# x's second load issued at the exponential, and the stage back to channels on four quarters with two staging buffers and eight banks

## The chip, the cores and the metric

One core of one Trainium2 chip runs the whole program in one launch. The metric is the device time in microseconds (us); lower is better. The kernel before was timed in three runs.

## The reference, cut to what matters

The input x has 16 images of 128 channels of 32 x 32. The first layer normalises x in groups, takes each of the 16 x 128 matrices of 32 x 32 through a matrix logarithm, subtracts the mean logarithm, and takes the matrix exponential. The result is added to x itself; then attention with the 32 largest scores and a gated set of four experts follow on the tokens.

```python
x = x + _L0_conv_ref(_gn(x), L0_conv_gamma, L0_conv_beta)
t = _to_tokens(x)
t = t + _L1_attn_ref(_ln_t(t), ...)
t = t + _L1_ffn_ref(_ln_t(t), ...)
x = _from_tokens(t, x)
```

The change lies at the plus sign of the first line: the exponentials are laid out by 32 x 32 blocks, x by channels, and the stage called back to channels turns the first into the layout of the second and adds.

## The kernel before, in words

The program is a row of blocks; each block gives every engine its own list of instructions, and all engines meet at its end before the next one starts. The order is: constants, normalise, spectral constants, into blocks, eigen, take the logarithm (to line 764), exponential (lines 777 to 955), back to channels (lines 958 to 1008), load the weights (POOL's fills at lines 1109 to 1115, loads at line 1132), attention and experts.

Two large tiles of 128 partitions x 16 x 1024 floats (8 MB each) carry the first layer. `mem.odd` holds x, then the matrices under work, then the logarithms, and at the end the exponentials. `mem.even` holds the normalised x and then the eigenvectors; its last readers are lines 715 and 731, in the logarithm. From there to the stage back to channels nothing touches it.

**The exponential.** 128 tiles of 128 x 128 floats pass through a pipeline of ten steps on TensorE (line 951, each a set of sixteen 32 x 32 products), with ScalarE emptying the banks (line 916) and VectorE making the sums (lines 862 to 890). The helper `through` writes out the first 11 slots and the last ones instruction by instruction and puts the middle into a loop. SyncE issues two small loads there, gamma and beta (lines 831 and 832), and is then idle until the end of the block. VectorE's first instruction waits for both loads, its loop over tiles for POOL's small unit matrices (line 842).

**Back to channels.** SyncE issues the load of x from memory into `mem.even` (line 972) at the stage's start. Then a loop over four quarters (four images each):

- ScalarE copies a quarter of `mem.odd`, 128 x 4096 floats, rearranged into `stage[0]` (line 981), and then waits until TensorE has turned all eight banks of the quarter.
- TensorE waits for the copy and turns it in 32 products of 128 x 128 with the identity, four to a bank (line 993). Each float32 product shows in the trace as two weight loads and two matmuls, so a quarter is 64 of each. It uses banks 0 to 3 in turn: from the fifth bank on it waits until VectorE has added the bank four before. At the end of a quarter it waits for all eight adds.
- VectorE waits for the load of x once, and then for each bank (line 1003), and adds the bank, 128 x 512, to the matching part of `mem.even` (line 1007).
- POOL waits for the load of x (line 976).

`mem.work` has room for two quarters; only the first is used as a stage. PSUM has eight banks.

Lines 2105 to 2107 call the two stages:

```python
exponential(nc, mem, dram["gamma"], dram["beta"])
mem.work = first.enter_context(nc.sbuf_tensor("work2", [P, 2, HB * PAIRS * S], F32))
back_to_channels(nc, mem, x_dram)
```

The program's only engine with a queue for its own transfers here is SyncE; the profile calls instructions of that queue SPq. Instructions themselves are brought in by transfers too, which the profile lists as queues of the kind "instruction" (q8 and q14).

Of the kernel before, what the change touches and what calls it, by code (L numbers as in the profile page):

```python
# [12 lines left out]
P = 128  # L13
B = 16
S = 32
# [8 lines left out]
QUADS = B // 4  # L24
# [26 lines left out]
def hold(eng, sem, value):  # L51

    eng.wait_ge(sem, value)
    eng.sem_inc(Passed.sem, 1)


class Passed:
    sem = None
# [14 lines left out]
def constants(nc, mem):  # L73

    with ExitStack() as ctx:
        filled = ctx.enter_context(nc.semaphore("filled"))
        block = ctx.enter_context(nc.Block())

        @block.gpsimd
        def _(pool):  # L80
            nc.gpsimd.memset(mem.ident[:], 0.0).then_inc(filled, 1)
            nc.gpsimd.memset(mem.group[:], 1.0 / (GROUP * N)).then_inc(filled, 1)
            nc.gpsimd.memset(mem.quad_mean[:], 0.0).then_inc(filled, 1)
            nc.gpsimd.memset(mem.eps_gn[:], EPS_GN).then_inc(filled, 1)
            hold(pool, filled, 4)
            nc.gpsimd.affine_select(out=mem.ident[:], in_=mem.ident[:], compare_op=ALU.not_equal, fill=1.0,
                                    base=0, pattern=[[-1, P]], channel_multiplier=1).then_inc(filled, 1)

            gv = mem.group[:].rearrange("p (g c) -> p g c", c=GROUP)
            nc.gpsimd.affine_select(out=gv, in_=gv, compare_op=ALU.is_ge, fill=0.0, base=0,  # L90
                                    pattern=[[-GROUP, P // GROUP], [0, GROUP]], channel_multiplier=1).then_inc(filled, 1)
            hold(pool, filled, 6)
            nc.gpsimd.affine_select(out=gv, in_=gv, compare_op=ALU.is_ge, fill=0.0, base=GROUP - 1,
                                    pattern=[[GROUP, P // GROUP], [0, GROUP]], channel_multiplier=-1).then_inc(filled, 1)

            for d in range(-3, 4):
                hold(pool, filled, 7 + d + 3)
                nc.gpsimd.affine_select(out=mem.quad_mean[:], in_=mem.quad_mean[:], compare_op=ALU.not_equal,
                                        fill=1.0 / (B * P), base=S * d, pattern=[[-1, P]],
                                        channel_multiplier=1).then_inc(filled, 1)  # L100
# [673 lines left out]
EXP_LEAD = EXP_DEPTH + 2  # L774


def exponential(nc, mem, gamma_dram, beta_dram):


    with ExitStack() as ctx:  # L780
        def sem(name):
            return ctx.enter_context(nc.semaphore(name))
# [11 lines left out]
        loaded, step, eyes = sem("gb_loaded"), sem("exp_step"), sem("eyes")  # L794
# [4 lines left out]
        banks = [b[:, 0:EXP_W] for b in mem.banks]  # L799
        logs = mem.odd[:].rearrange("p m n -> p (m n)")  # L800
        block = ctx.enter_context(nc.Block())
        c = TAYLOR
# [26 lines left out]
        @block.sync  # L829
        def _(sp):  # L830
            sp.dma_start(scal[:, 0:1], gamma_dram.partition_broadcast(P)).then_inc(loaded, 16)
            sp.dma_start(scal[:, 1:2], beta_dram.partition_broadcast(P)).then_inc(loaded, 16)

        @block.gpsimd
        def _(pool):
# [119 lines left out]
            through(pe, slot)  # L955


def back_to_channels(nc, mem, x_dram):

    with ExitStack() as ctx:  # L960
        def sem(name):
            return ctx.enter_context(nc.semaphore(name))

        loaded, staged, turned, added = sem("x_again"), sem("back_staged"), sem("back_turned"), sem("back_added")
        stage = [mem.work[:, n].rearrange("p (c k) -> p c k", k=P) for n in range(2)]
        powers = mem.odd[:].rearrange("p (g b) n -> p g (b n)", g=QUADS)
        banks = mem.banks
        block = ctx.enter_context(nc.Block())

        @block.sync  # L970
        def _(sp):
            sp.dma_start(mem.even[:], x_dram).then_inc(loaded, 16)

        @block.gpsimd
        def _(pool):
            hold(pool, loaded, 16)

        @block.scalar
        def _(act):
            with act.Fori(0, QUADS) as g:  # L980
                nc.scalar.activation(stage[0].rearrange("p c k -> p k c"),
                                     powers[:, g, :].rearrange("p (k c) -> p k c", c=S), ACT.Copy).then_inc(staged, 1)
                act.wait_ge(turned, g * 8 + 8)

        @block.tensor
        def _(pe):
            with pe.Fori(0, QUADS) as g:
                hold(pe, staged, g + 1)
                for b in range(8):
                    if b >= 4:  # L990
                        hold(pe, added, g * 8 + b - 3)
                    for n in range(4):
                        last = nc.tensor.matmul(banks[b % 4][:, P * n:P * n + P], stage[0][:, 4 * b + n, :], mem.ident[:],
                                                start=True, stop=True)
                    last.then_inc(turned, 1)
                hold(pe, added, g * 8 + 8)

        @block.vector
        def _(dve):
            dve.wait_ge(loaded, 16)  # L1000
            with dve.Fori(0, QUADS) as g:
                for b in range(8):
                    dve.wait_ge(turned, g * 8 + b + 1)

                    d = mem.even[:, bass.ds(g * 4, 4), :].rearrange("p q (r c) -> p q r c", c=S)[:, :, :, 4 * b:4 * b + 4]
                    d = d.rearrange("p q r c -> p c q r")
                    nc.vector.tensor_tensor(d, d, banks[b % 4][:].rearrange("p (c q r) -> p c q r", c=4, q=4),
                                            ALU.add).then_inc(added, 1)


HEADS = 8
# [1063 lines left out]
def hybrid_kernel(nc, dram, out):  # L2075
    x_dram = dram["x"].rearrange("b c h w -> c b (h w)")
    out_dram = out.rearrange("b c h w -> c b (h w)")
    with ExitStack() as ctx:
        mem = Memory()

        def sb(name, shape, dtype=F32):
            return ctx.enter_context(nc.sbuf_tensor(name, shape, dtype))

        mem.flag = ctx.enter_context(nc.sbuf_tensor("flag", [1, 1], mybir.dt.int32))
        mem.ident = sb("ident", [P, P])
        mem.group = sb("group", [P, P])
        mem.quad_mean = sb("quad_mean", [P, P])
        mem.eps_gn = sb("eps_gn", [P, 1])
        mem.even = sb("even", [P, B, N])
        mem.psum = ctx.enter_context(nc.psum_tensor("psum", [P, 8, 512], F32))  # L2090
        mem.banks = [mem.psum[:, i, :] for i in range(8)]
        Passed.sem = ctx.enter_context(nc.semaphore("passed"))
        constants(nc, mem)
        with ExitStack() as first:
            mem.odd = first.enter_context(nc.sbuf_tensor("odd", [P, B, N], F32))
            normalise(nc, mem, x_dram)
            with ExitStack() as spectral:
                e = Spectral(nc, mem, lambda name, shape, dtype=F32:
                             spectral.enter_context(nc.sbuf_tensor(name, shape, dtype)))
                spectral_constants(nc, mem, e)  # L2100
                into_blocks(nc, mem, e)
                e.open_tiles(lambda name, shape, dtype=F32: spectral.enter_context(nc.sbuf_tensor(name, shape, dtype)))
                eigen(nc, mem, e)
                take_logarithm(nc, mem, e)
            exponential(nc, mem, dram["gamma"], dram["beta"])
            mem.work = first.enter_context(nc.sbuf_tensor("work2", [P, 2, HB * PAIRS * S], F32))
            back_to_channels(nc, mem, x_dram)
        w = Tiles(sb)
        load_weights(nc, mem, w, dram)
        attention_and_experts(nc, mem, w, out_dram)  # L2110
# [21 lines left out]
```

## Time and profile before

| what | us |
|---|---|
| median of three runs | 9082.76 |
| lowest and highest | 9075.89, 9084.97 |
| the profiled execution, its own time | 9074.8 |
| its span | 9073.1 |
| busy: PE, DVE, ACT, POOL | 7923.9, 5380.0, 3778.8, 1947.5 |
| exponential, from its first small load to its last copy | 3916.5 to 4639.3 |
| back to channels, from the issue of x's load to the last add | 4639.5 to 4725.0 |
| loading the weights, from POOL's first fill to the next stage's first matmul | 4725.7 to 4758.2 |

The span runs from the first instruction to the last; the execution's own time lies 1.7 us above it. PE is TensorE's matmuls, PEld its weight loads, DVE VectorE, ACT ScalarE, POOL GpSimd. A row of the timeline gives start, duration and the idle time before it with what ended it in brackets; with several instructions in a row (x6) the duration is that of all of them together. "issue" is idle time in which the engine waited for nothing that the profile shows.

### The profile page before, as it was taken

What the parts mean: (1) busy time and instruction counts of PE and PEld (TensorE: products, weight loads), DVE (VectorE), ACT (ScalarE), POOL (GpSimd) and SP (SyncE); (2) the same over time, 40 slices, a digit from 0 to 9 for tenths busy, and PEclk for the clock granted to TensorE, in tenths of its full rate; (3) what the DMA queues carried; (4) which work ended last, traced back from release to release, by engine and by line L of the source; (5) the groups of instructions that cost most, each with busy time, mean ns of one, the idle gap of its engine ahead of it and who ended that gap; (6) DMA issues with size and microseconds to landing.
All of it is one profiled execution on the core that took longest, in us unless ns stands there. A gap on an engine that the chain in (4) does not pass through costs nothing. (4 is left out here: it accounts for less than half of the span.)

```text
span 9073.1 us, 601301 instructions
## 1 busy us (share of the span) xinstructions
PE 7923.9 (87%) x265196; PEld 4270.7 (47%) x265196; DVE 5380.0 (59%) x15117; ACT 3778.8 (42%) x7262; POOL 1947.5 (21%) x2028
## 2 busy tenths in 40 slices
PE   3999999999999778668856999999999999999998
PEld 2677777777777666557741222222222222222222
DVE  4677777777777546643324555555555555555553
ACT  3455555555555334324422333333334333333333
POOL 1455555555555334300000000000000000000000
PEclk9999999999999889779967999999999999999999
DMA  0000000000000000000010000000000000000000
GB/s 37 1 0 0 0 0 0 0 0 0 0 0 0 0 0 0 1 1 0 0 42 14 15 17 17 12 16 15 13 17 15 17 15 12 17 10 17 15 17 5
DMA packets 58886, 82.10 MB, mean 9 GB/s; under 512 B 26101, under 2 KB 27706, under 8 KB 58426
## 3 DMA queue, kind: packets, MB, share of 16 engines
q1 hardware_dynamic: 58426, 76.45, 3.2%
q8 instruction: 229, 3.75, 0.2%
q14 instruction: 231, 1.89, 0.1%
HBM read 17.63 MB, written 8.39 MB: 3 GB/s over the span
## 5 line engine op out<-in xcount | busy, mean ns | idle before, releaser
L1867 DVE MAX8 w_best<-psum 128x8 f32<-128x128 f32 x8192 | 1725.0, 283 | 1301.9 <-PE psum L1409 1300.5
L1850 ACT ACTIVATE w_exp<-psum 128x512 f32<-128x512 f32 x2048 | 1220.1, 596 | 2291.7 <-PE psum L1418 2289.4
L1428 PE MATMUL psum<-w_exp,w_v 128*32 128x512 f32 x4096 | 2087.6, 608 | 3.0 <-ACT w_inverse L1461 2.7
L1409 PE MATMUL psum<-w_k,w_q 96*128 96x512 bf16 x2048 | 637.3, 394 | 239.7 <-DMA w_k<-w_parts 145.0
L1418 PE MATMUL psum<-w_q,w_k 99*128 99x512 bf16 x2048 | 798.2, 390 | 1.4 <-ACT w_q L1443 1.4
L499 PE MATMUL psum<-e_prod_u,e_j 32*32 32x64 f32 x49152 | 769.8, 215 | 30.5 <-ACT e_prod_u L579 25.1
L499 PEld LDWEIGHTS psum<-e_prod_u,e_j 32*32 32x32 f32 x49152 | 708.0, 105 | 183.2 <-issue 183.2
L1409 PEld LDWEIGHTS psum<-w_k,w_q 96*128 96x128 bf16 x2048 | 123.7, 98 | 1071.4 <-issue 1071.2
L1428 PEld LDWEIGHTS psum<-w_exp,w_v 128*32 128x32 f32 x4096 | 276.0, 108 | 716.8 <-issue 716.8
L653 POOL TENSOR_TENSOR e_diag<-odd,e_eye 128x512 f32<-128x512 f32 x384 | 488.0, 1271 | 559.4 <-PE psum L473 521.3
L547 ACT ACTIVATE e_square<-e_off 128x512 bf16<-128x512 f32 x384 | 242.1, 630 | 844.0 <-POOL e_off L657 844.0
L1418 PEld LDWEIGHTS psum<-w_q,w_k 99*128 99x128 bf16 x2048 | 204.1, 100 | 790.8 <-issue 675.3
L382 PE MATMUL psum<-e_mix,e_zs 32*32 32x32 f32 x49152 | 509.8, 196 | 61.6 <-issue 60.0
L606 DVE TENSOR_TENSOR e_j<-e_rest,psum 128x512 f32<-128x512 f32 x384 | 264.0, 687 | 470.4 <-PE psum L382 470.4
L382 PEld LDWEIGHTS psum<-e_mix,e_zs 32*32 32x32 f32 x49152 | 477.5, 107 | 108.7 <-issue 108.4
L382 PE MATMUL psum<-e_x 32*32 32x32 f32 x49152 | 505.1, 195 | 14.6 <-issue 14.3
L382 PE MATMUL psum<-e_j,e_a_fixed 32*32 32x32 f32 x49152 | 495.9, 194 | 19.6 <-issue 12.7
L951 PE MATMUL psum<-power 32*32 32x32 f32 x28672 | 391.5, 205 | 118.6 <-issue 111.6
L382 PEld LDWEIGHTS psum<-e_j,e_a_fixed 32*32 32x32 f32 x49152 | 462.5, 104 | 62.6 <-issue 28.1
L663 POOL TENSOR_TENSOR e_x_eye<-e_x,e_eye 128x512 f32<-128x512 f32 x384 | 487.8, 1270 | 2.4 <-DVE e_x L634 2.4
L657 POOL TENSOR_TENSOR e_off<-odd,e_not_eye 128x512 f32<-128x512 f32 x384 | 487.9, 1271 | 0.0
L382 PEld LDWEIGHTS psum<-e_x 32*32 32x32 f32 x49152 | 472.5, 106 | 29.6 <-issue 16.3
(268 smaller groups left out, 10889.3 us busy)
## 6 DMA issues: line engine op xcount, KB each, us to landing
w_q<-w_parts SPq DMA_DIRECT2D x768, 32.0 KB, 2.0
w_k<-w_parts SPq DMA_DIRECT2D x768, 32.0 KB, 2.0
odd<-in_x SPq DMA_DIRECT2D x1, 8192.0 KB, 23.1
even<-in_x SPq DMA_DIRECT2D x1, 8192.0 KB, 23.2
out<-w_t SPq DMA_DIRECT2D x16, 512.0 KB, 2.6
w_hid<-in_fc SPq DMA_DIRECT2D x2, 256.0 KB
w_wo<-in_wo SPq DMA_DIRECT2D x8, 8.0 KB
w_wq<-in_wq SPq DMA_DIRECT2D x1, 64.0 KB
```

The costliest lines, as they stand in the source:

```text
L382: last = nc.tensor.matmul(bank[rows, cols], left[rows, cols], right[rows, cols], start=True, stop=True)
L499: last = nc.tensor.matmul(halves(e.pair[:, k // HALF, :])[rows, :, to], e.j[rows, cols], e.prod_u[rows, :, cols], start=True, stop=True)
L606: nc.vector.tensor_tensor(e.j[:], e.rest[:], banks[TURN], ALU.add).then_inc(turned, 1)
L653: nc.gpsimd.tensor_tensor(as_matrices(e.diag[:]), as_matrices(e.a_at(t)), over_matrices(e.eye[:]), ALU.mult)\
L657: nc.gpsimd.tensor_tensor(as_matrices(e.off[:]), as_matrices(e.a_at(t)), over_matrices(e.not_eye[:]), ALU.mult)\
L663: nc.gpsimd.tensor_tensor(as_matrices(e.x_eye[:]), as_matrices(e.x[:]), over_matrices(e.eye[:]), ALU.add)\
L951: last = nc.tensor.matmul(banks[EXP_BANK[n]][rows, S * k:S * k + S], left[rows, k, :], right[rows, k, :], start=True, stop=True)
L1409: last = nc.tensor.matmul(banks[base + k], w.q[0:DEPTH, 4 * g + j, q0:q0 + P], w.k[0:DEPTH, 4 * g + j, half(k)], start=True, stop=True)
L1418: nc.tensor.matmul(banks[4 + x % 2], w.k[0:DEPTH + SHIFT_ROWS, 4 * g + j, P * kt:P * kt + P], w.q[0:DEPTH + SHIFT_ROWS, 4 * g + j, half(qb ...
L1428: nc.tensor.matmul(banks[7][slot(j), :], w.v[:, kt, 4 * g + j, :], w.exp[x % 4][:], start=(kt == 0), stop=(kt == KT - 1)).then_inc(s.weigh ...
L1850: nc.scalar.activation(w.exp[x % 4][:], banks[4 + x % 2], ACT.Exp).then_inc(s.exp_done, 1)
L1867: last = nc.vector.max(w.best[:, i, o, :], banks[o // 4][:, P * (o % 4):P * (o % 4) + P])
```

## The change

x's load moves from the stage back to channels into the exponential, behind the two small loads of SyncE; its semaphore is made before the stage and is passed on as `mem.x_again`. POOL's wait for it goes. In the stage back to channels the loops over quarters are written out four times. ScalarE fills two stages in turn and waits only from the third quarter on, for the quarter two before. TensorE uses all eight banks, waits for the add eight banks before, and no longer waits at a quarter's end. VectorE ends with a wait for its own last add.

```diff
--- before.py
+++ after.py
@@ -774,7 +774,7 @@
 EXP_LEAD = EXP_DEPTH + 2
 
 
-def exponential(nc, mem, gamma_dram, beta_dram):
+def exponential(nc, mem, gamma_dram, beta_dram, x_dram):
 
 
     with ExitStack() as ctx:
@@ -830,6 +830,7 @@
         def _(sp):
             sp.dma_start(scal[:, 0:1], gamma_dram.partition_broadcast(P)).then_inc(loaded, 16)
             sp.dma_start(scal[:, 1:2], beta_dram.partition_broadcast(P)).then_inc(loaded, 16)
+            sp.dma_start(mem.even[:], x_dram).then_inc(mem.x_again, 16)
 
         @block.gpsimd
         def _(pool):
@@ -955,57 +956,50 @@
             through(pe, slot)
 
 
-def back_to_channels(nc, mem, x_dram):
+def back_to_channels(nc, mem):
 
     with ExitStack() as ctx:
         def sem(name):
             return ctx.enter_context(nc.semaphore(name))
 
-        loaded, staged, turned, added = sem("x_again"), sem("back_staged"), sem("back_turned"), sem("back_added")
+        staged, turned, added = sem("back_staged"), sem("back_turned"), sem("back_added")
         stage = [mem.work[:, n].rearrange("p (c k) -> p c k", k=P) for n in range(2)]
         powers = mem.odd[:].rearrange("p (g b) n -> p g (b n)", g=QUADS)
         banks = mem.banks
         block = ctx.enter_context(nc.Block())
 
-        @block.sync
-        def _(sp):
-            sp.dma_start(mem.even[:], x_dram).then_inc(loaded, 16)
-
-        @block.gpsimd
-        def _(pool):
-            hold(pool, loaded, 16)
-
         @block.scalar
         def _(act):
-            with act.Fori(0, QUADS) as g:
-                nc.scalar.activation(stage[0].rearrange("p c k -> p k c"),
+            for g in range(QUADS):
+                if g >= 2:
+                    act.wait_ge(turned, (g - 1) * 8)
+                nc.scalar.activation(stage[g % 2].rearrange("p c k -> p k c"),
                                      powers[:, g, :].rearrange("p (k c) -> p k c", c=S), ACT.Copy).then_inc(staged, 1)
-                act.wait_ge(turned, g * 8 + 8)
 
         @block.tensor
         def _(pe):
-            with pe.Fori(0, QUADS) as g:
+            for g in range(QUADS):
                 hold(pe, staged, g + 1)
                 for b in range(8):
-                    if b >= 4:
-                        hold(pe, added, g * 8 + b - 3)
+                    if g * 8 + b >= 8:
+                        hold(pe, added, g * 8 + b - 7)
                     for n in range(4):
-                        last = nc.tensor.matmul(banks[b % 4][:, P * n:P * n + P], stage[0][:, 4 * b + n, :], mem.ident[:],
+                        last = nc.tensor.matmul(banks[b][:, P * n:P * n + P], stage[g % 2][:, 4 * b + n, :], mem.ident[:],
                                                 start=True, stop=True)
                     last.then_inc(turned, 1)
-                hold(pe, added, g * 8 + 8)
 
         @block.vector
         def _(dve):
-            dve.wait_ge(loaded, 16)
-            with dve.Fori(0, QUADS) as g:
+            dve.wait_ge(mem.x_again, 16)
+            for g in range(QUADS):
                 for b in range(8):
                     dve.wait_ge(turned, g * 8 + b + 1)
 
-                    d = mem.even[:, bass.ds(g * 4, 4), :].rearrange("p q (r c) -> p q r c", c=S)[:, :, :, 4 * b:4 * b + 4]
+                    d = mem.even[:, g * 4:g * 4 + 4, :].rearrange("p q (r c) -> p q r c", c=S)[:, :, :, 4 * b:4 * b + 4]
                     d = d.rearrange("p q r c -> p c q r")
-                    nc.vector.tensor_tensor(d, d, banks[b % 4][:].rearrange("p (c q r) -> p c q r", c=4, q=4),
+                    nc.vector.tensor_tensor(d, d, banks[b][:].rearrange("p (c q r) -> p c q r", c=4, q=4),
                                             ALU.add).then_inc(added, 1)
+            dve.wait_ge(added, 8 * QUADS)
 
 
 HEADS = 8
@@ -2092,6 +2086,7 @@
         Passed.sem = ctx.enter_context(nc.semaphore("passed"))
         constants(nc, mem)
         with ExitStack() as first:
+            mem.x_again = first.enter_context(nc.semaphore("x_again"))
             mem.odd = first.enter_context(nc.sbuf_tensor("odd", [P, B, N], F32))
             normalise(nc, mem, x_dram)
             with ExitStack() as spectral:
@@ -2102,9 +2097,9 @@
                 e.open_tiles(lambda name, shape, dtype=F32: spectral.enter_context(nc.sbuf_tensor(name, shape, dtype)))
                 eigen(nc, mem, e)
                 take_logarithm(nc, mem, e)
-            exponential(nc, mem, dram["gamma"], dram["beta"])
+            exponential(nc, mem, dram["gamma"], dram["beta"], x_dram)
             mem.work = first.enter_context(nc.sbuf_tensor("work2", [P, 2, HB * PAIRS * S], F32))
-            back_to_channels(nc, mem, x_dram)
+            back_to_channels(nc, mem)
         w = Tiles(sb)
         load_weights(nc, mem, w, dram)
         attention_and_experts(nc, mem, w, out_dram)
```

## Rows read from the trace of the kernel before

**Rows 1.** The page: TensorE's granted clock in tenths, in 40 slices of 227 us.
```profile
PEclk9999999999999889779967999999999999999999
```

**Rows 2.** Timeline, 4638 to 4726: start us, us, engine, line, operation, count, idle before.
```profile
4639.53 0.38 SPq L972 DMA_DIRECT2D even<-in_x  x1
4639.72 7.14 ACT L981 ACTIVATE work<-odd 128x4096 f32 x1 [0.45 <-PEq L780]
...
4647.00 6.70 PE L993 MATMUL psum<-ident,work 128*128 128x128 f32 x32 [8.06 <-ACT work L981]
4663.04 6.34 DVE L1007 TENSOR_TENSOR even<-even,psum 128x512 f32 x6 [51.92 <-DMA even<-in_x]
...
4671.27 7.13 ACT L981 ACTIVATE work<-odd 128x4096 f32 x1 [24.42 <-PE psum L993]
...
4678.55 9.88 PE L993 MATMUL psum<-ident,work 128*128 128x128 f32 x64 [7.64 <-ACT work L981]
4680.77 1.17 DVE L1007 TENSOR_TENSOR even<-even,psum 128x512 f32 x1 [8.59 <-PE psum L993]
4682.45 1.16 DVE L1007 TENSOR_TENSOR even<-even,psum 128x512 f32 x1 [0.51 <-PE psum L993]
4684.11 6.36 DVE L1007 TENSOR_TENSOR even<-even,psum 128x512 f32 x6 [0.50 <-PE psum L993]
...
4718.60 6.39 DVE L1007 TENSOR_TENSOR even<-even,psum 128x512 f32 x6 [0.17 <-PE psum L993]
4725.66 0.31 POOL L1109 MEMSET w_wo<- 128x256 f32 x1 [805.47 <-POOLq L960]
```

**Rows 3.** Waits, 4636 to 4765: us in total, times, longest us.
```profile
DVE even L1007 <- DMA even<-in_x: 51.9, 1, 51.9
ACT work L981 <- PE psum L993: 45.0, 3, 24.4
```

**Rows 4.** Windows: us, busy of PE, PEld, DVE, ACT, POOL, granted clock, DMA share, GB/s.
```profile
4650.00:4653.00 3.00, 3.00 (x16) 3.00 (x16) 0.00 (x0) 0.00 (x0) 0.00 (x0) 0.50 1.03 411
4653.00:4654.00 1.00, 0.70 (x6) 0.51 (x5) 0.00 (x0) 0.00 (x0) 0.00 (x0) 0.97 1.01 406
...
4720.00:4722.00 2.00, 2.00 (x21) 2.00 (x20) 2.00 (x3) 0.00 (x0) 0.00 (x0) 1.00 0.00 0
```

**Rows 5.** Line 1007 by itself: duration in ns, least, median and most.
```profile
L1007 DVE TENSOR_TENSOR even<-even,psum x32: 1097/1154/1320, 4663.0 to 4723.8; 128x512 f32 x32
```

**Rows 6.** Timeline, 3915 to 3945, the head of the exponential.
```profile
3916.90 0.43 SPq L832 DMA_DIRECT2D scal<-in_beta  x1
...
3919.48 0.15 DVE L851 TENSOR_SCALAR scal<-scal 128x1 f32<-128x1 f32 x1 [4.13 <-DMA scal<-in_beta]
...
3920.31 0.35 DVE L862 SCALAR_TENSOR_TENSOR a_first<-odd,scal,offset 128x128 f32<-128x128 f32 x1
...
3935.70 1.43 PE L951 MATMUL psum<-power 32*32 32x32 f32 x89 [2.07 <-issue]
...
3939.54 0.58 PE L951 MATMUL psum<-a_first 32*32 32x32 f32 x26 [1.67 <-issue]
...
3943.54 1.07 PE L951 MATMUL psum<-power 32*32 32x32 f32 x63 [2.09 <-issue]
```

**Rows 7.** DMA, 3918 to 3942: packets, MB, share of 16 engines.
```profile
q8 instruction: 5, 0.08, 1.6%
```

**Rows 8.** DMA, 4636 to 4670: all packets, and x's load with KB and us to landing.
```profile
DMA packets 2066, 8.41 MB, mean 247 GB/s; under 512 B 16, under 2 KB 16, under 8 KB 2064
...
even<-in_x SPq DMA_DIRECT2D x1, 8192.0 KB, 23.2
```

**Rows 9.** Windows, the exponential's written-out head; columns as in rows 4.
```profile
3920.00:3996.00 76.00, 41.71 (x2394) 37.82 (x2397) 24.08 (x91) 16.05 (x63) 0.19 (x1) 0.50 0.02 4
```

**Rows 10.** DMA, 4760 to 9073, the attention: packets, MB, share of 16 engines.
```profile
q8 instruction: 154, 2.52, 0.2%
```

**Rows 11.** Waits of TensorE, 4760 to 9073: the longest of all.
```profile
PE psum L1409 <- DMA w_k<-w_parts: 145.0, 16, 33.2
```

## The prediction

> **What bounds the kernel now.** The page first: TensorE's granted clock is near full except in the slices around the exponential's ends and the stage changed here [rows 1]. That stage is one hundredth of the span of 9073.1 us, so shares of busy time over the whole span say nothing of it; the timeline of the stage does. It runs from 4639.53, where x's load is issued, to 4724.99, the end of the last add (4718.60 + 6.39), and 0.67 us later POOL starts the next block [rows 2]. That is 85.5 us in which every engine mostly waits for another. Read the waits next: VectorE stands until x has landed, and ScalarE stands 45.0 us in three waits for TensorE [rows 3]. So the stage is two chains one after the other. First, x's load: 23.2 us to landing [rows 8], VectorE starts only at 4663.04, and TensorE, with four banks, has stopped at 4653.7. Then three quarters in series, (4724.99 - 4671.27) / 3 = 17.9 us each: copy 7.13, turn, add; no copy can start before the quarter ahead is turned [rows 2].
>
> **Part 1, x's load is gone from the stage.** VectorE's first add can follow TensorE's first bank. In the later quarters it starts 2.2 us after TensorE does (4678.55 to 4680.77) [rows 2]; TensorE's start at 4647.0 stays, so the first add comes at 4649.2.
>
> **Part 2, two stages and eight banks.** I run the new order by hand with the durations of rows 2 and 4.
>
> - ScalarE: quarters 0 and 1 back to back, 4639.7 to 4646.9 and to 4654.0.
> - TensorE: at the half clock (1.2 GHz) it does 16 matmuls in 3 us, hence a bank (8 of them) in some 1.6 us; at the full clock (2.4 GHz) 21 in 2 us, a bank in 0.8 us. It went from one level to the other at about 4653, after unbroken work since 4647.0 [rows 4]. So four banks of quarter 0 at the low level to 4653.6, four at the high one to 4656.8; quarter 1, staged since 4654.0, follows at once to 4663.3.
> - ScalarE quarter 2: needs quarter 0 turned, 4656.9 to 4664.1; quarter 3 needs quarter 1 turned, so it follows at once, to 4671.4. TensorE then turns quarter 2 from 4664.2 and quarter 3 from 4671.5.
> - VectorE: the first three adds come at 1.66 us, as at 4680.77, 4682.45 and 4684.11 [rows 2], and the fourth starts at about 4654.1. Six adds in a row took 6.36 us with the last one's 1.1 in it, so the pitch is 1.05 us [rows 2, 5]. From the fourth add on VectorE is the slowest: 8.4 us to a quarter against 7.1 (ScalarE) and 6.4 (TensorE). The end is 4654.1 + 28 x 1.055 + 1.1 = 4684.7.
>
> Is VectorE ever starved? Quarter 0's adds end at 4659.4, when quarter 1's first bank (4658.2) is there; quarter 1's end at 4667.9 against 4665.6; quarter 2's at 4676.3 against 4672.9. No. Against 4724.99 the stage gains **40.3 us**. ScalarE's waits and TensorE's end-of-quarter waits go with no one late behind them; what is late next is VectorE's own chain of adds. If ScalarE or TensorE lost 2.3 us in quarter 2, VectorE would start to wait; that is the cover of all that I cost at nothing here.
>
> **Part 3, small things in the stage.** POOL's wait goes; POOL stood at the block's end anyway. VectorE's new last wait is for its own last add, ahead of a meeting that already came 0.67 us after it: 0 to 0.1 us. Writing the loops out makes TensorE's list 512 instructions of the product instead of 128 in a loop. New instructions have to be fetched, and the exponential shows that: with its head written out, TensorE stood 2.07, 1.67 and 2.09 us at 3935.7, 3939.5 and 3943.5, about every 3.9 us for some 90 to 130 matmuls [rows 6]. In the stage as many matmuls take 10 us or more, so the next fetch is hidden behind them: 0, with one exposed fetch, 2.1 us, as the upper end, less than the slack above for one and less than 3 us for two.
>
> **Part 4, x's load in the exponential.** SyncE issues it some 0.5 us behind beta's, at about 3917.4, and nothing else waits in its queue until the block ends. It runs from about 3918 to 3941. Two things lie there.
>
> Beta first. VectorE got it at 3919.48, and made its first tile at 3920.31 [rows 6]. Beta is ahead in the same queue; I take 0, and the upper end is the whole load, 22 us, if its landing were held.
>
> Then TensorE's instruction fetches. In the head of the exponential TensorE works 41.7 us of 76, at the half clock, and the rest is mostly those stalls [rows 9]; they lie on the path, since every tile goes through TensorE. The queue of its instructions brought five pieces between 3918 and 3942, at 1.6% of 16 engines over 24 us: 6.1 us, 1.2 us each [rows 7]. No row of before shows how a fetch fares against the 8 MB load, which fills all engines (406 to 411 GB/s) [rows 4]. Lower bound 0. Upper bound: the first fetch after the load's start, near 3924, waits until its end: 16 us, and those behind it find the engines empty. Between them the nearest row is the fetch's own 1.2 us: if the load and the fetch share an engine evenly, a fetch takes twice as long. Four of the five fall wholly under the load: 4 x 1.2, **5 us** lost.
>
> The Trainium skill ("Runtime: NRT & Kernel Launch", Instruction fetch mechanics) says that crossing into the next block of instructions is mostly hidden. By it this term would be zero and the sum 5 us lower. The stalls of 1.67 to 2.09 us [rows 6] say otherwise here, so I keep the term.
>
> **The sum.** -40.3 + 5 = -35.3 us. On the profiled execution's 9074.8 us that is 9039.5. The profiled execution lay 8 us under the median of the runs, 9082.76, and the gain does not depend on that, so the median should be 9047.
>
> **The rivals.**
>
> A. **The fetch waits behind a batch of x's packets**, not beside one. 2048 packets of x over 16 engines in 22 us are 128 to an engine, 0.17 us each [rows 8]; if some 15 stand ahead of each fetch, it is 2.6 us x 4, 10 us, and up to the 16 of the bound. Gain 24 to 30, time 9053 to 9059. For it: a transfer already handed to an engine is queued there. Against it: nothing in rows. The Trainium skill speaks for it ("DMA: Bandwidth & Descriptors", Queues, rings and completion order): an engine drains a whole packet of 9 to 17 descriptors from one ring before it turns to the next; by that 1.5 to 2.9 us a fetch as an estimate, 6 to 12 in all. No row here shows it. Chance 0.2.
>
> B. **TensorE stays at the half clock.** Then 32 banks x 1.65 are 53 us from 4647.0, and with the last add the end is 4701.5: gain 23.5, less 5, time 9064. Against it: in quarter 0, and in each later burst, the clock rose while TensorE worked without a pause, and the new order leaves no pause until 4663. Chance 0.04.
>
> C. **The adds slow down** with ScalarE's copy and TensorE beside them: at the longest duration, 1.32 in place of 1.15 [rows 5], 28 x 0.17 are 5 us; gain 30, time 9052. Chance 0.07.
>
> D. **The gain is no gain**: beta's landing is held for the load's 22 us, gain 18 or less, time 9065 to 9083. Against it: beta is issued first. Chance 0.04.
>
> E. **Slower.** The written-out loops put all later code of TensorE elsewhere against the pieces in which it is fetched. The attention brings 154 pieces [rows 10], 9.6 to each of 16 images. TensorE's longest wait there is for a transfer of keys [rows 11], and none of its waits in that list ends in "issue", so the fetches are hidden now. A newly exposed one costs 2 us [rows 6]; two to an image are 32 x 2 = 64 us, time 9111. It decides from 18 newly exposed ones (35 us, gain gone) and is measurably slower from 27. Against it: 4313 us over 154 pieces are 28 us of work to a piece, against the 3.9 us in which the exponential's head gets one. Chance 0.02.
>
> **How the numbers follow.** My forecast, part 4 at 2 to 8 us, has 0.63, with its own range of 9038 to 9053. The low end 9034 is the gain with no loss at all (9042), 2 us better on the adds and 6 us of scatter, as the three runs lay 9 us apart. The high end 9064 takes in A, C and B. About 0.2%, 18 us, is what a measurement of this kernel can tell from no change: faster than 9064.6 in all cases but D and E, 0.93; D and scatter 0.05; E 0.02.
>
> **What would show it.** The stage from its first copy to its last add is 45 us, where it was 85.3. VectorE's wait for x is gone, its adds are in one run of about 29 at 1.05 us. ScalarE has one wait of some 3 us. TensorE's clock rises near 4653 of the old time and stays. In the head of the exponential the stalls of "issue" grow from 2 to some 3 us while x is loading. From 3996 on to the stage, and from POOL's first fill on, all durations are as before. Wrong would be: adds with gaps between quarters, a clock of 0.50 after the first quarter, a stall of over 5 us in the exponential's head, or a stage 40 us shorter with a total that is not.

## The result and the profile after

The changed kernel takes 9046.48 us (median of six runs, 9042.74 to 9050.84), the kernel before 9083.59 (six runs, 9075.89 to 9086.64). The ratio is 0.996, 95% interval 0.9949 to 0.9971: 37 us faster (26 to 46 by the interval), where 35 were forecast.

The profiled execution has this head and this clock (the page):

```profile
span 9044.6 us, 600800 instructions
...
PEclk9999999999999889779977999999999999999999
```

Timeline of the new stage, to compare with [rows 2]:

```profile
4650.06 14.25 ACT L976 ACTIVATE work<-odd 128x4096 f32<-128x4096 f32 x2 [0.29 <-PEq L780]
...
4657.34 17.18 PE L987 MATMUL psum<-ident,work 128*128 128x128 f32 x128 [7.90 <-ACT work L976]
4659.49 1.17 DVE L1000 TENSOR_TENSOR even<-even,psum 128x512 f32<-128x512 f32 x1 [38.41 <-PE psum L987]
4661.12 1.13 DVE L1000 TENSOR_TENSOR even<-even,psum 128x512 f32<-128x512 f32 x1 [0.47 <-PE psum L987]
4662.83 32.16 DVE L1000 TENSOR_TENSOR even<-even,psum 128x512 f32<-128x512 f32 x30 [0.58 <-PE psum L987]
4667.41 15.21 ACT L976 ACTIVATE work<-odd 128x4096 f32<-128x4096 f32 x2 [3.10 <-PE psum L987]
...
4675.40 14.89 PE L987 MATMUL psum<-ident,work 128*128 128x128 f32 x128 [0.88 <-ACT work L976]
...
4695.81 0.31 POOL L1103 MEMSET w_wo<- 128x256 f32 x1 [772.24 <-POOLq L961]
```

ScalarE copies two quarters in a row, waits 3.1 us, and copies two more. VectorE's last 30 adds are one row without idle time: 4662.83 + 32.16 = 4694.99 is the end. From the first copy that is 44.9 us, where it was 4724.99 - 4639.72 = 85.3.

The waits of the same stretch, for [rows 3]; VectorE's wait for x is gone, and so is most of ScalarE's:

```profile
DVE even L1000 <- PE psum L987: 39.5, 3, 38.4
...
ACT work L976 <- PE psum L987: 3.1, 1, 3.1
```

The granted clock in the stage (windows, columns as in rows 4): half while the first banks are turned, full from then on, with the engine nearly unbroken.

```profile
4657.40:4663.00 5.60, 5.60 (x27) 5.60 (x28) 2.46 (x3) 5.60 (x1) 0.00 (x0) 0.51 0.00 0
...
4666.00:4668.00 2.00, 2.00 (x21) 2.00 (x20) 2.00 (x3) 0.59 (x1) 0.00 (x0) 1.00 0.00 0
```

And the head of the exponential (timeline of TensorE), which pays for it. These are the same instructions as in the kernel before:

```profile
3924.18 0.65 PE L952 MATMUL psum<-a_first 32*32 32x32 f32 x32 [4.72 <-DVE a_first L863]
...
3933.38 0.47 PE L952 MATMUL psum<-a,a_second 32*32 32x32 f32 x18 [2.81 <-issue]
...
3939.75 0.54 PE L952 MATMUL psum<-power 32*32 32x32 f32 x22 [3.94 <-issue]
...
3946.50 1.43 PE L952 MATMUL psum<-power 32*32 32x32 f32 x89 [4.55 <-issue]
...
3950.33 0.58 PE L952 MATMUL psum<-a_first 32*32 32x32 f32 x26 [1.67 <-issue]
```

A stall is idle time of TensorE that ends in "issue". The fourth is 1.67 us in both kernels. The third, ahead of the row of 89 products, was 2.07 [rows 6] and is 4.55; the second, ahead of the 22 products, grew from 1.45 to 3.94 and the first from 0.34 to 2.81 (the rows of before for these two stand in this fence):

```profile
3927.53 0.48 PE L951 MATMUL psum<-a,a_second 32*32 32x32 f32 x18 [0.34 <-issue]
...
3931.43 0.54 PE L951 MATMUL psum<-power 32*32 32x32 f32 x22 [1.45 <-issue]
```

Each of the three is 2.5 us longer, 7.4 in all. The packets of q8, the queue that brings TensorE's instructions, say where these microseconds lie (starts and durations from the DMA packets of the two traces; the last two rows set them against the rows of TensorE):

| fetches of the head | before | after |
|---|---|---|
| starts at | 3924.9, 3928.8, 3933.1, 3937.0 | 3930.8, 3937.2, 3944.0, 3947.8 |
| lasts | 1.33, 1.16, 1.27, 1.27 | 1.04, 1.11, 1.11, 1.10 |
| from its end to TensorE's going on | 1.3, 1.5, 1.3, 1.3 | 1.5, 1.4, 1.4, 1.5 |
| from TensorE's going on to the next fetch | 1.3, 1.7, 1.3 | 3.8, 4.2, 1.3 |

Every stall ends 1.3 to 1.5 us after a fetch, in both kernels, and the fetch itself is no longer than before. The two gaps ahead of a fetch that lie under the load (x's packets end at 3945.5) are each 2.6 us longer; the one behind it is not. The first fetch, too, starts 6.6 us after TensorE's first product where it was 4.1.

Put together, the two profiled executions differ like this:

| stretch | before | after | difference |
|---|---|---|---|
| to the issue of gamma's load | 3916.5 | 3919.9 | +3.4 |
| from there to the stage's first copy | 723.2 | 730.2 | +7.0 |
| stage, first copy to last add | 85.3 | 44.9 | -40.3 |
| last add to the end | 4348.1 | 4349.6 | +1.5 |
| span | 9073.1 | 9044.6 | -28.5 |

The first and the last row are code that the change leaves alone, and scatter: in three profiled executions of the changed kernel gamma's load was issued at 3919.9, 3918.6 and 3923.1, and the code behind the last add took 4349.6, 4339.5 and 4349.9 us. A cost of a few microseconds in these two stretches would not be seen. The medians, with a 37 us gain, are nearer to the two middle rows (-33.3) than this one pair of spans is.

One execution of an experiment, the profiled one of load_in_loop, took 11204 us at a mean granted clock of 0.649; its stages are not read below.

### The profile page after: what moved, and what is told of

It is laid out like the page before. It is cut to its first block and busy times, and to the rows that moved or that the text cites. A ratio compares the mean times of both kernels' runs of the same rounds, so it can differ in the third digit from the quotient of the medians.

```text
span 9044.6 us, 600800 instructions
## 1 busy us (share of the span) xinstructions
PE 7902.4 (87%) x264813; PEld 4264.2 (47%) x265196; DVE 5377.2 (59%) x15117; ACT 3783.5 (42%) x7262; POOL 1949.7 (22%) x2028
```

## The experiments

Twelve runs follow: nine other kernels, one of them twice, and the changed kernel twice more. Four things were open: how the 40 us split between the load and the stage, and within the stage between the staging buffers and the banks; what the 7 us in the exponential are; and whether they can be had back. The diffs are cut to the lines that matter; "exponential" below is the time from gamma's issue to the stage's first copy, "stage" that from the first copy to the last add.

**The load and the stage, one without the other.**

```diff
 load_only: in exponential, as in the change; the stage as before
+            sp.dma_start(mem.even[:], x_dram).then_inc(mem.x_again, 16)
 stage_only: the new stage, in back_to_channels
+        @block.sync
+        def _(sp):
+            sp.dma_start(mem.even[:], x_dram).then_inc(mem.x_again, 16)
```

> Only x's load is moved, the stage stays as before (one staging buffer, four banks, loops). Expected: the exponential 730 us; in the stage the first quarter is turned in one go, and the second copy starts near 17 us after the first, not 31.5, so the stage is 71 us from the first copy to the last add; gain 14.4 less 7.2, 7 us in all. Rival (the load is what bounds the stage): the stage goes down by the 23 us of the load, gain 16.

Measured: 9077.91 us against 9079.9, ratio 0.9999 (0.9989 to 1.0008): no gain that can be told from none, where 7 us were expected. In its profile the exponential takes 733.5 us and the stage 70.1. The rows (timeline) show the three later quarters as serial as ever, 17.1 us apart:

```profile
4652.18 7.13 ACT L974 ACTIVATE work<-odd 128x4096 f32 x1 [0.44 <-PEq L780]
...
4669.27 7.14 ACT L974 ACTIVATE work<-odd 128x4096 f32 x1 [9.96 <-PE psum L986]
...
4686.35 7.14 ACT L974 ACTIVATE work<-odd 128x4096 f32 x1 [9.94 <-PE psum L986]
...
4714.60 7.67 DVE L1000 TENSOR_TENSOR even<-even,psum 128x512 f32 x7 [0.51 <-PE psum L986]
```

> Only the stage is new, x's load stays at its start. Expected: the exponential 723 us; VectorE starts when x has landed, 23.5 us into the stage, and adds 32 banks in one run at 1.07 us, 34.3 us, so that the last add ends 58 us after the load's issue; gain 27.5 us. Rival (the two parts only work together): TensorE has stood with its eight banks full and its clock is down when the adds begin, at 1.65 us to a bank the adds would take 41 us, gain 21.

Measured: 9051.62 us, ratio 0.9973 (0.9964 to 0.9982), a gain of 28 us by the medians and 16 to 33 by the interval; 27.5 were expected. Exponential 723.2 us; VectorE stands until x is there and then adds all 32 banks without a gap, so the last add ends 57.4 us after the load's issue:

```profile
4644.57 0.38 SPq L972 DMA_DIRECT2D even<-in_x  x1
...
4668.21 33.71 DVE L1003 TENSOR_TENSOR even<-even,psum 128x512 f32<-128x512 f32 x32 [51.78 <-DMA even<-in_x]
```

So the stage's new order is worth 28 us alone, the earlier load 15 us in the stage less 10 in the exponential (some 5 by the profile, 2 by the medians), and together they give 37. Why the load alone gives so little: with x there from the start, the first quarter still takes the 17.1 us of every serial quarter, where it took 31.5 before, and that is all that the stage wins.

**Staging buffers and banks.**

```diff
 one_stage
-                if g >= 2:
-                    act.wait_ge(turned, (g - 1) * 8)
-                nc.scalar.activation(stage[g % 2]...
+                if g >= 1:
+                    act.wait_ge(turned, g * 8)
+                nc.scalar.activation(stage[0]...
                 ... (TensorE reads stage[0] too)
 four_banks
-                    if g * 8 + b >= 8:
-                        hold(pe, added, g * 8 + b - 7)
+                    if g * 8 + b >= 4:
+                        hold(pe, added, g * 8 + b - 3)
-                        last = nc.tensor.matmul(banks[b]...
+                        last = nc.tensor.matmul(banks[b % 4]...
                 ... (VectorE adds banks[b % 4])
```

> The changed kernel with one staging buffer, eight banks kept: each copy waits until the quarter before is turned. Expected: copy 7.1 and turning in series, four times some 17 us as in the last quarters before, the stage 70 us from the first copy to the last add where the changed kernel has 45. Rival (the banks bring the gain): under 50 us.

Measured: 9070.76 us in one run (before: 9081.59). The copies start 17.3 to 17.6 us apart again, and the stage takes 71.4 us:

```profile
4649.99 7.14 ACT L976 ACTIVATE work<-odd 128x4096 f32<-128x4096 f32 x1 [0.29 <-PEq L780]
...
4667.60 7.16 ACT L976 ACTIVATE work<-odd 128x4096 f32<-128x4096 f32 x1 [10.47 <-PE psum L987]
```

> The changed kernel with two staging buffers and four banks in turn. VectorE is the slowest from its fourth add on, and four banks ahead are 4.3 us of adds, so it should not starve inside a quarter; at a quarter's start TensorE is held more. Expected: the stage 45 to 47 us, at most 2 us longer than with eight. Rival (the banks bring the gain): 60 us or more.

Measured: 9047.66 us in one run, and the stage 44.1 us, even a little shorter than with eight banks: from 4653.40 to 4662.84 + 34.67 = 4697.51.

```profile
4653.40 14.40 ACT L976 ACTIVATE work<-odd 128x4096 f32<-128x4096 f32 x2 [0.29 <-PEq L780]
4662.84 34.67 DVE L1000 TENSOR_TENSOR even<-even,psum 128x512 f32<-128x512 f32 x32 [37.33 <-PE psum L987]
```

The 0.8 us are not shown to come from the banks: TensorE's granted clock was full from 4663.5 here, 2.8 us after its first product, and in the changed kernel from about 4663, 5.6 us after; load_in_loop2 below, with eight banks, has a stage of 44.0. The second staging buffer is worth 26 us, the four more banks nothing, with two staging buffers (44.1 against 44.9) and with one (71.4, and 70.1 in load_only with four banks). Both of these runs are single ones, and read by the stage: with VectorE the slowest, four banks ahead of it are enough.

**Where the 7 us go: the load moved into the loop.**

```diff
+            sp.wait_ge(out[EXP_STAGES - 1], 16)
             sp.dma_start(mem.even[:], x_dram).then_inc(mem.x_again, 16)
```

> x's load waits for the 16th finished tile of the exponential, when TensorE is in the loop and fetches no instructions. Theory (the 7 us lost in the exponential are fetches of TensorE's written-out head that stand behind x's packets): the exponential is back at 723 us, the three long stalls of the head (2.8, 3.9, 4.6 us) are back at 0.3, 1.5 and 2.1, the stage stays at 45, the time is 7 us under the changed kernel. Rival 1 (x's writes into SBUF slow the engines, or the longer program does it): the loss moves into the loop, 730 us as in the changed kernel. Rival 2 (the exponential's length scatters by 7 us from run to run): no order between the two.

> The changed kernel as it is, for comparison on the same chip. In its first profile the exponential took 730.2 us from gamma's load to the next block (723.0 before) and the stage 44.9 us from the first copy to the last add (85.3 before). Expected again: 730 and 45, a time 36 to 38 us under the kernel before.

Measured: the kernel with the load in the loop takes 9042.11 us (median of its other five executions), ratio to before 0.9954 (0.9941 to 0.9968), the changed kernel 9047.56 us and 0.9969 (0.9956 to 0.9981). For the stages both ran once more:

> The kernel with x's load behind the 16th finished tile once more, since its first profile was taken in an execution of 11204 us with a mean granted clock of 0.649, from which no stage can be read. Theory: the exponential 723 us, the stage 45; time 7 us under the changed kernel and 43 under the kernel before. Rival (the loss only moves into the loop): 730 us.

> The changed kernel once more beside the one with the load in the loop: the exponential 730 to 733 us, the stage 45, time 36 us under the kernel before.

Measured: 9037.02 us (five runs, 9032.52 to 9048.63) with the load in the loop, 9048.89 (9043.42 to 9053.71) for the changed kernel; ratios to before 0.9951 (0.9937 to 0.9964) and 0.9962 (0.9949 to 0.9976). The intervals of the ratios overlap; the order is the same both times. Taken together, ten executions with the load in the loop have a median of 9037.3, eleven of the changed kernel 9048.9, and the profiles show where the difference comes from. In the loop's kernel the exponential takes 721.4 us against 729.4 in the changed kernel's (732.5 in after_again's), and the stalls of the head are near those of before (timeline of TensorE):

```profile
3933.23 0.54 PE L953 MATMUL psum<-power 32*32 32x32 f32 x22 [1.19 <-issue]
...
3937.23 1.43 PE L953 MATMUL psum<-power 32*32 32x32 f32 x89 [1.81 <-issue]
```

While x is loading (first row, 350 GB/s) TensorE starts 1548 products in 24 us, and 1507 in 24 us just after it (second row), so that the load costs nothing there (windows):

```profile
4061.00:4085.00 24.00, 19.93 (x1548) 17.90 (x1547) 8.68 (x35) 11.37 (x43) 0.00 (x0) 0.93 0.90 350
4090.00:4114.00 24.00, 19.62 (x1507) 17.57 (x1508) 9.80 (x40) 11.39 (x43) 0.00 (x0) 0.93 0.00 0
```

No packet of q8 falls into these 48 us, nor into the 584 us of the loop around them. Rival 1 of the expectation, that the loss moves into the loop, is out. So is rival 2, that the exponential scatters by as much: in the three profiled executions without the load in its head (before, stage_only, load_in_loop2) it takes 721.4 to 723.2 us, in the seven with all of it there, behind gamma's and beta's, 729.4 to 733.5. This version is 44 us under the kernel before, which was timed beside it.

**How a fetch meets the load.**

```diff
 x_in_2k
+            for n in range(2):
+                sp.dma_start(mem.even[:, :, 512 * n:512 * n + 512], x_dram[:, :, 512 * n:512 * n + 512])...
             ... (VectorE waits for 32 in both of these kernels)
 x_half_early
+            sp.dma_start(mem.even[:, 0:8, :], x_dram[:, 0:8, :]).then_inc(mem.x_again, 16)
+            sp.wait_ge(out[EXP_STAGES - 1], 16)
+            sp.dma_start(mem.even[:, 8:16, :], x_dram[:, 8:16, :]).then_inc(mem.x_again, 16)
```

> x's load in the head of the exponential in two loads of rows of 2 KB in place of one of 4 KB. The three stalls of TensorE under the load are each 2.5 us longer than before. Theory A (a fetch waits behind a fixed number of x's packets, some 15 of 0.17 us): with packets half as long, 1.2 to 1.3 us more each. Theory B (it waits behind a fixed number of bytes, or gets a share of the engine by bytes): still 2.5 us each.

Measured: the packets are twice as many and half as long, and the three stalls are 3.63, 3.92 and 4.26 us, 11.8 in all against 11.3; the exponential takes 730.6. Theory A had the sum at 7.6. The rows (DMA over the load in x_in_2k, then two of TensorE's stalls):

```profile
DMA packets 4419, 8.45 MB, mean 331 GB/s; under 512 B 319, under 2 KB 319, under 8 KB 4415
```

```profile
3941.44 0.54 PE L953 MATMUL psum<-power 32*32 32x32 f32 x22 [3.92 <-issue]
3947.90 1.43 PE L953 MATMUL psum<-power 32*32 32x32 f32 x89 [4.26 <-issue]
```

So the wait is not for a fixed number of packets. Between Theory B's two forms, a fixed number of bytes ahead of the fetch or a share of the engine by bytes, the changed kernel's own DMA rows decide, over the same 24 us as [rows 7] counted from gamma's load:

```profile
DMA packets 2273, 8.45 MB, mean 352 GB/s; under 512 B 221, under 2 KB 221, under 8 KB 2269
...
q8 instruction: 3, 0.05, 0.8%
```

Three fetches in place of five, at 0.8% of 16 engines over 24 us: 3.1 us, 1.0 us each, where it was 1.2. A fetch is not longer under the load; it begins later, as the table of fetches has it packet by packet. That is a wait ahead of it, worth 2.5 us or, at 24 us for 512 KB an engine, an estimate of some 53 KB of x. A fixed time, whatever x's bytes, would fit both runs as well: both loaded x at the same rate, and no run changed that. What the fetch waits for (packets already taken up by the engine, reads under way, or something else) stays open.

> Images 0 to 7 of x are loaded in the head of the exponential, images 8 to 15 from the 16th finished tile on. The first load lasts some 12 us, from 1 us before the first tile. Theory (fetches under the load are late, nothing else): one of the three stalls is 2.5 us longer, perhaps two, the exponential 726 us. Rival (a fixed cost of having the load there): 730 us.

Measured: 9035.36 us in one run, the exponential 727.9 us. The first stall is 3.06 us (0.34 without a load), the next two 1.18 and 2.35, near the 1.45 and 2.07 of before. One fetch was late, as the theory has it; of the 4.7 us that the exponential is longer than before, 2.0 are not explained by it, so 727.9 lies between the theory's 726 and the rival's 730. After_again's exponential, too, is 2.3 us longer than the changed kernel's first one with the same stalls. A total 11 us under the changed kernel's in a single run is no more than scatter allows.

**Who waits behind whom.**

```diff
 x_first: x's load ahead of gamma's and beta's in SyncE's queue
 small_on_act: x's load alone in SyncE's queue, the small ones in ScalarE's
+            act.dma_start(scal[:, 0:1], gamma_dram.partition_broadcast(P)).then_inc(loaded, 16)
+            act.dma_start(scal[:, 1:2], beta_dram.partition_broadcast(P)).then_inc(loaded, 16)
```

> x's load is issued ahead of gamma's and beta's in the same queue. Theory (each engine takes a queue's packets in their order): beta lands behind all of x, some 25 us after its issue and not 2.7, VectorE's first tile is 22 to 23 us late, and TensorE's fetches then meet no load any more: the exponential 745 us. Rival (the small loads pass x's): 730 us.

Measured: 9049.15 us in one run, the exponential's block 743.6 us from x's issue. Both small loads land when x does (x 23.2 us after its issue, they at 3936.8 and 3937.3; DMA rows, then the timeline), and TensorE's head has stalls of 0.34, 1.47 and 2.36 us, since its fetches come after the load. The exponential is some 13 us longer than the changed kernel's, and the total is not: gamma's load was issued 6 us earlier and the code behind the stage was 3.6 us shorter in this execution, both in code that the edit leaves alone, so a single total says little here.

```profile
even<-in_x SPq DMA_DIRECT2D x1, 8192.0 KB, 23.2
scal<-in_gamma SPq DMA_DIRECT2D x1, 0.5 KB, 22.6
scal<-in_beta SPq DMA_DIRECT2D x1, 0.5 KB, 14.0
```

```profile
3914.17 9.04 SPq L832 DMA_DIRECT2D scal<-in_gamma  x1
...
3937.29 0.15 DVE L852 TENSOR_SCALAR scal<-scal 128x1 f32<-128x1 f32 x1 [24.70 <-DMA scal<-in_beta]
```

> x's load is first in SyncE's queue, and gamma's and beta's are issued from ScalarE's queue at the same time. Theory (a transfer of another queue waits only behind what the engine has already taken up of x, the 2.5 us that a fetch waits): beta lands at most 2.5 us later than 2.7 us after its issue, the exponential 730 to 733 us. Rival (a transfer of any queue waits for all of x): 745 us or more.

Measured: 9047.23 us in one run, the exponential 734.3 us. Neither all of x nor 2.5 us: gamma lands after 6.9 us and beta after 8.0 (2.2 and 2.6 before), 4.7 and 5.4 us late, about two of the waits that a fetch has one of.

```profile
scal<-in_gamma ACTq DMA_DIRECT2D x1, 0.5 KB, 6.9
scal<-in_beta ACTq DMA_DIRECT2D x1, 0.5 KB, 8.0
```

In one queue the small loads landed with the large one; from another queue they got in between. The size that I gave was half of it, the exponential is above the 730 to 733 expected, and why it is twice a fetch's wait wasn't tried.

## Why the prediction was right, and which term was off

**Parts 1 and 2, the stage.** -40.3 us forecast, -40.3 measured in the profile. The steps: first add 2.2 us behind TensorE's start (4657.34 to 4659.49, 2.15), the clock up in the middle of quarter 0 and then kept, ScalarE's one wait 2.9 us (3.10 measured), VectorE without a gap to the end. That the two agree to 0.1 us is luck: small errors cancelled. The pitch of the adds is (32.16 - 1.1) / 29 = 1.07 us in place of 1.055, half a microsecond over the stage, rival C in a small size; and the fourth add began half a microsecond sooner after the first copy than forecast (13.9 us, 14.4 forecast), since the third add already had no wait behind it. ScalarE's last two copies take 15.21 us together, 7.7 each in place of 7.13 (four_banks and stage_only show a single one beside the adds at 7.70); VectorE, being the slowest, hid them, and the slack of 2.3 us in quarter 2 was enough for that 1 us.

**Part 3.** The written-out loops cost nothing: TensorE's 128 matmuls of quarters 0 and 1 are one row of 17.18 us without idle time, and a fetch that starts at 4679.0, in the middle of the row of 14.89 us, does not interrupt it either: it is hidden, as forecast. VectorE's last wait is within 0.82 us from last add to POOL's first fill, 0.67 before.

**Part 4, beta.** Zero, as forecast: from gamma's issue to the first tile 3923.69 - 3919.87 = 3.82 us, before 3.81. What protects it is its place ahead of x; x_first shows the price of the other order, a first tile 20 us later.

**Part 4, the fetches, is the term that was mis-sized**, 5 us against 7.0 to 7.4. The step "if the load and the fetch share an engine evenly, a fetch takes twice as long" failed: a fetch takes no longer, it begins 2.5 us later, and three of them do, not four, since each delay spreads them out: 3 x 2.5 = 7.4 against 4 x 1.2 = 4.8. The error per fetch was a factor of two, and one fetch too many in the count made it 2 us in the sum: luck again. The sign that was named, stalls that grow to some 3 us, is off with it (2.8, 3.9 and 4.6). Rival A had a wait ahead of the fetch and 2.6 us for each, but four of them, and a count of packets, which x_in_2k speaks against; its chance of 0.2 was too low against a form of the forecast for which no row spoke either.

With this term at its measured size the sum is -33, not -35. The measured medians are 37 apart; that they lie nearer to the forecast than to the mended sum is scatter and no merit.

The Trainium skill ("DMA: Bandwidth & Descriptors", Queues, rings and completion order) has an engine drain a whole packet of 9 to 17 descriptors before it turns to another ring, 1.5 to 2.9 us as an estimate with x's 4 KB pieces. The 2.5 us lie within it. With 2 KB pieces (about 0.09 us each, 256 to an engine in some 24 us) the same count would give 0.8 to 1.6 us as an estimate, and the stalls stayed where they were: that would take some 27 pieces, more than the count that the page calls typical and under the 64 that it gives as the ceiling. A fixed count is out; whether the packet grew with smaller pieces no run shows. Its other rule, that crossing into the next block of instructions is mostly hidden ("Runtime: NRT & Kernel Launch", Instruction fetch mechanics), would have put this term at zero; the three rows of TensorE's stalls (2.81, 3.94 and 4.55 us) speak against it for this head, and the stage's written-out loops agree with it (the fetch at 4679.0 costs nothing).

**The rivals that fell.** B: the clock is 1.00 from 4663 on. D: the load lies behind beta. E: from the last add to the end 4348.1 and 4349.6 us, while the changed kernel's three profiled executions differ there by 10 us, so the moved code cost nothing that shows, and the 64 us of the rival are out.

## What to carry to other kernels

A load that is hidden from the engine that waits for it can still meet the transfers that bring in instructions. Put it where the busy engine runs a loop, not where its code is written out: here that was a single wait ahead of the load, worth some 8 us in the exponential. And before buffers are doubled everywhere, ask which engine will be the slowest in the new order: the second staging buffer gave 26 us, the four more banks none.

## What the runs showed of the hardware that I had not expected

- An instruction fetch beside an 8 MB load is not slower (1.0 to 1.1 us each; 0.9 to 1.3 in the heads without it), it begins 2.5 us later, and that does not shrink when the load's packets are halved from 4 KB to 2 KB (three stalls of 11.3 us in all, then 11.8).
- A small load issued behind the 8 MB one in the same queue landed when the large one did, and its issue alone held SyncE's queue for 9.04 us (0.35 before). From another engine's queue it landed 4.7 to 5.4 us late (one run each).
- While 350 GB/s went into SBUF, the exponential's loop ran no slower (1548 products begun in 24 us, 1507 in the 24 us behind it).
- ScalarE's copies of 128 x 4096 take 7.7 us beside VectorE's unbroken adds and TensorE's products at the full clock, and 7.13 alone; the adds go from 1.055 to 1.07 us. Which of the two engines slows the copy is not shown.
